# Loading W1 and W2 by 128-partition blocks from SyncE alone, and sharing the rounding of W1's first block with VectorE

## What is computed

```python
hidden = concat([cond, cond])                  # (4, 512)
x_mean = mean(x, axis=1, keepdims=True)        # over the 1024 rows of a batch
fused  = concat([x, x_mean, hidden])           # 1536 features for each row
out    = x + relu(fused @ W + b)               # W is (1536, 512)
```

## Time and profile before

| | us |
|---|---|
| median of the runs | 104.74 |
| the profiled execution | 105.25 |
| its span on the core | 103.1 |
| TensorE busy | 97.4 |
| VectorE busy | 81.7 |
| ScalarE busy | 47.3 |
| GpSimd busy | 41.0 |
| the first product that counts starts | 7.07 |
| `mean_bias(1)` starts | 40.57 |
| the last product starts | 99.50 |

### The profile page before, as it was taken

The page is one execution under the profiler, slowest core; times in us unless marked ns, Lnnn a source line. Parts: engine busy times, 40 slices in busy tenths (PEclk is TensorE's granted clock), DMA queues, the critical chain, the costliest instruction groups (busy, mean ns, idle before and its releaser), DMA issues.

```text
span 103.1 us, 1694 instructions
## 1 busy us (share of the span) xinstructions
PE 97.4 (95%) x523; PEld 78.3 (76%) x523; DVE 81.7 (79%) x146; ACT 47.3 (46%) x116; POOL 41.0 (40%) x37
## 2 busy tenths in 40 slices
PE   5989999999999898999999999999999999999970
PEld 2349999778888585888888886888888886888960
DVE  3173869979879999999999994999999994839660
ACT  3277426875606549777487100874744004610000
POOL 1029700000000000999857700468577059992000
PEclk9999999999999999999999999999999999999997
DMA  2999999999999999999999999300591690199995
GB/s 63 290 306 273 220 214 216 235 235 218 233 270 253 209 224 221 225 225 224 219 296 349 309 282 251 97 0 0 111 267 29 144 253 14 39 279 263 230 330 183
DMA packets 34990, 21.39 MB, mean 207 GB/s; under 512 B 1572, under 2 KB 32680, under 8 KB 34984
## 3 DMA queue, kind: packets, MB, share of 16 engines
q1 hardware_dynamic: 33400, 20.13, 85.4%
q10 hardware_dynamic: 1584, 1.18, 3.8%
HBM read 12.91 MB, written 8.39 MB: 207 GB/s over the span
## 4 chain that ended last, share of the span: by engine, by line
PE 57%; SPq 18%; DMA 10%; DVE 7%; issue 3%; ACT 1%; DVEq 0%
PE ps_y L457 46%; DMA xa<-in_x_dram 10%; SPq L162 9%; PE ps_y L558 4%; PE ps_y L560 4%; PE ps_y L559 4%; SPq L166 2%; SPq L170 2%; DVE w2x L361 2%; DVE ps_xt L331 2%; SPq L158 2%; SPq L195 2%; ACT xh L257 1%; DVE xl L337 1%; SPq L190 1%
## 5 line engine op out<-in xcount | busy, mean ns | idle before, releaser
L232 POOL TENSOR_TENSOR xa<-xa,back 128x512 f32 x28 | 35.6, 1295 | 45.8 <-DVE back L344 45.8
L457 PE MATMUL ps_y<-xh,w1h 128*128 (+2 forms) x128 | 43.7, 368 | 0.3 <-ACT w1h L250 0.3
L457 PE MATMUL ps_y<-xl,w1h 128*128 (+2 forms) x128 | 43.1, 363 | 0.0
L457 PE MATMUL ps_y<-xh,w1l 128*128 (+2 forms) x128 | 42.9, 363 | 0.0
L257 ACT ACTIVATE xh<-ps_xt 128x512 fp32r<-128x512 f32 (+1 forms) x36 | 19.7, 549 | 21.1 <-DVE ps_xt L331 21.1
L331 DVE STREAM_TRANSPOSE ps_xt<-xa 128x512 f32<-128x512 f32 (+1 forms) x36 | 22.3, 643 | 5.8 <-DMA xa<-in_x_dram 5.4
L457 PEld LDWEIGHTS ps_y<-xh,w1h 128*128 128x128 f32 x128 | 22.6, 188 | 5.6 <-issue 0.8
L457 PEld LDWEIGHTS ps_y<-xh,w1l 128*128 128x128 f32 x128 | 22.6, 189 | 3.9
L337 DVE TENSOR_TENSOR xl<-ps_xt,xh 128x512 fp32r<-128x512 f32 (+1 forms) x36 | 22.2, 618 | 4.1 <-ACT xh L257 4.1
L457 PEld LDWEIGHTS ps_y<-xl,w1h 128*128 128x128 f32 x128 | 22.7, 189 | 3.5
L275 ACT ACTIVATE relu_t<-ps_y,bias 128x512 f32<-128x512 f32 x20 | 13.5, 686 | 16.5 <-DVE bias L378 15.0
(11 more groups left out here) (34 smaller groups left out, 35.8 us busy)
## 6 DMA issues: line engine op xcount, KB each, us to landing
xa<-in_x_dram SPq DMA_DIRECT2D x28, 256.0 KB, 7.2
out_dram<-xa SPq DMA_DIRECT2D x28, 256.0 KB, 4.1
w<-in_L_cond_W_dram SPq DMA_DIRECT2D x4, 256.0 KB, 7.6
w<-in_L_cond_W_dram SPq DMA_DIRECT2D x2, 512.0 KB, 8.3
w<-in_x_dram SPq DMA_DIRECT2D x4, 256.0 KB, 6.2
out_dram<-w SPq DMA_DIRECT2D x3, 256.0 KB, 3.2
xa<-in_x_dram SPq DMA_DIRECT2D x4, 128.0 KB, 3.6
xa<-in_x_dram ACTq DMA_DIRECT2D x4, 128.0 KB, 4.0
```

What stands on the lines that cost most here:

```text
L232: nc.gpsimd.tensor_tensor(rows, rows, back[:, t], ALU.add).then_inc(added, 1)
L457: return nc.tensor.matmul(ps_y[:, t, ls], lhs, rhs, start=start, stop=stop, skip_group_check=True)
```

## The change

- `load_w1` and `load_w2` take a block k in place of a list of quadrants. One transfer of 256 KB fills all 128 partitions of block k, from `wv[0, :, :, k]`, an array of 4 by 32 rows of 512 numbers; the rows of one j follow each other, and those of the next j begin 128 rows further on. There are four transfers for W1 (12 before) and four for W2 (as before, but these had one j and all k each).
- SP alone issues W1 and the second part of x0. ACT issues only its half of x0's first part.
- x1 is issued ahead of the condition, and VectorE takes the transpose of the condition behind x1's pieces.
- Each block of W1 has a semaphore of its own, so block 2 no longer waits for block 3.
- ScalarE rounds only the first two of the four tiles of W1's block 0, and does so between x0's first two pieces; VectorE copies the other two (`tensor_copy`, 128x256). TensorE waits for these ahead of its tile 2, and GpSimd for both parts.
- `WARM` is 12 in place of 14.

```diff
-WARM = 14
+WARM = 12
...
+    DVE_T = NK // 2
...
-        def load_w1(eng, first, end, quadrants):
-            for j in quadrants:
-                eng.dma_start(w1[Q * j:Q * j + Q, first:end], wv[0, j, :, first:end]).then_inc(w1_landed[first], 16)
-
-        def load_w2(eng, quadrants):
-            for j in quadrants:
-                eng.dma_start(w2[Q * j:Q * j + Q], wv[1, j]).then_inc(w2_landed, 16)
+        def load_w1(eng, k):
+
+            eng.dma_start(w1[:, k], wv[0, :, :, k]).then_inc(w1_landed[k], 16)
+
+        def load_w2(eng, k):
+            eng.dma_start(w2[:, k], wv[1, :, :, k]).then_inc(w2_landed, 16)
...
             load_x0(sp, 0, LOW)
-            load_w1(sp, 0, 1, LOW)
-            load_w1(sp, 1, 2, LOW)
-            load_w1(sp, 2, NK, LOW)
-            load_x0(sp, 1, LOW)
+            for k in range(NK):
+                load_w1(sp, k)
+            load_x0(sp, 1, ORDER)
+            load_x(sp, 1, ORDER)
             sp.wait_ge(cond_zeroed, 1)
...
-            load_x(sp, 1, ORDER)
             load_x(sp, 2, ORDER)
-            load_w2(sp, ORDER)
+            for k in range(NK):
+                load_w2(sp, k)
...
             for k in range(NK):
-                pool.wait_ge(w1_landed[min(k, NK - 2)], 16 * NQ)
+                pool.wait_ge(w1_landed[k], 16)
                 pool.wait_ge(w1h_ready, k + 1)
+                if k == 0:
+                    pool.wait_ge(w1h_rest_ready, 1)
...
             nc.scalar.activation(act_warm[:], ones[:, 0:1], ACT.Relu)
-            load_w1(act, 0, 1, HIGH)
-            load_w1(act, 1, 2, HIGH)
-            load_w1(act, 2, NK, HIGH)
-            load_x0(act, 1, HIGH)
 
             def w1_high(k):
-                act.wait_ge(w1_landed[min(k, NK - 2)], 16 * NQ)
-                nc.scalar.activation(as_tiles(w1h[:, k]), by_tile(w1[:, k]), ACT.Copy).then_inc(w1h_ready, 1)
+                act.wait_ge(w1_landed[k], 16)
+                ts = slice(0, NK if k else DVE_T)
+                nc.scalar.activation(as_tiles(w1h[:, k])[:, ts], by_tile(w1[:, k])[:, ts], ACT.Copy).then_inc(w1h_ready, 1)
...
-            x_high(0)
-            x_high(1)
-            w1_high(0)
-            w1_high(1)
-            for k in range(2, NK):
+            for k in range(NK):
                 x_high(k)
                 w1_high(k)
...
             turn_x(0)
-            turn_and_split(0, pieces_to(1))
+            turn_x(1)
+            dve.wait_ge(w1_landed[0], 16)
+            nc.vector.tensor_copy(as_tiles(w1h[:, 0])[:, DVE_T:NK], by_tile(w1[:, 0])[:, DVE_T:NK]).then_inc(w1h_rest_ready, 1)
+            x_low(0)
+            turn_x(2)
+            turn_and_split(1, 2)
+            turn_and_split(2, pieces_to(1))
+            turn_x(pieces_to(1))
+            turn_and_split(pieces_to(1), pieces_to(H))
 
             dve.wait_ge(cond_landed, 16 * NQ)
             nc.vector.transpose(cond_t[:], cond_c[:].rearrange("p m k -> p k m")).then_inc(cond_spread, 1)
-            turn_x(pieces_to(1))
-            turn_and_split(pieces_to(1), pieces_to(H))
...
                     for t in range(NK):
+                        if half == 0 and k == 0 and t == DVE_T:
+                            pe.wait_ge(w1h_rest_ready, 1)
                         mm(t, ls, w1h[:, k, t], xh[:, 0, k, ls], start=(half == 0 and k == 0))
```

More of the change, by code:

```diff
@@ L135, in build @@
         x_landed = [sem(f"x_landed{g}") for g in range(G)]
-        w1_landed = [sem(f"w1_landed{k}") for k in range(NK - 1)]
+        w1_landed = [sem(f"w1_landed{k}") for k in range(NK)]
         w2_landed, w3_landed = sem("w2_landed"), sem("w3_landed")
@@ L140, in build @@
         warm_zeroed, cond_zeroed, ones_set = sem("warm_zeroed"), sem("cond_zeroed"), sem("ones_set")
-        w1h_ready, w1l_ready = sem("w1h_ready"), sem("w1l_ready")
+        w1h_ready, w1h_rest_ready, w1l_ready = sem("w1h_ready"), sem("w1h_rest_ready"), sem("w1l_ready")
         cond_spread, const_summed, const_ready = sem("cond_spread"), sem("const_summed"), sem("const_ready")
@@ L350, in mean_terms @@
                     nc.vector.tensor_tensor(xsum[:, 1], xsum[:, 0], xsum[:, 1], ALU.add).then_inc(halves_summed, 1)
-                    dve.wait_ge(w2_landed, 16 * NQ)
+                    dve.wait_ge(w2_landed, 16 * NK)
                     dve.wait_ge(halves_summed, 1)
```

## The result

Four runs of the changed kernel took 121.85 to 124.22 us, median 123.54; the kernel before, run beside it, 104.89. The ratio is 1.174, interval 1.168 to 1.179. Medians here are of all runs; ratios and their intervals leave out the runs over 1.5% above the fastest of their kernel. The profiled execution took 123.41 us (before 105.25), with a span of 121.6. The direction is the forecast one. The size is not: 18.65 us by the medians where 10 were forecast, outside the range.

A forecast was written before the change was run, and what follows sets the result against it. x3's landing, then fixed TensorE work, bounds the kernel. 4.2 + 22.4 + 13.3 + 0.5 lands x3 at 40.4, 9.5 later: 105.25 + 9.5 = 114.8, by the median 114.2, plus 0.5 for the clock: 114.7 (80% range 111.8 to 120.5).

The forecast's parts named there:

- Too few engines: Loads of W1 and W2: four runs in memory send each block through 4 engines, 64 KB each, not 16.
- 2.8 us a W block, 22.4 for eight: Loads ahead of x3: each W1 or W2 block takes 2.8 us on its four engines, eight 22.4 (21.5 to 28).
- twelve idle engines leave less crowding: Loads on the four engines: with the others idle or ahead, 2.8 us a W block and 3.8 a group of x.
- The group of x at 3.8 us: Loads up to x3: each group of x takes 3.8 us on one engine; 3.5 groups make 13.3 (12.2 to 16.8).
- The high end of my own working, 49.5: x3's landing: forecast at 40.4, range 38.4 to 49.5, against 30.9 before.
- the second rival: Loads: four engines, crowded as before, 3.5 us a block, 4.8 a group; up to 123.3, half way 119; 15 in 100.
- W3 lands near 43.5: W3's load behind x3, still on 16 engines: lands near 43.5 to 44, 43.5 taken; TensorE waits from 39.6.
- x3 decides: Mean product of batch 1: x3's landing plus 9.7 gives 50.1, TensorE's path through W3 49.1; x3 sets it by 1 us.
- The clock at 0.5 us on even chances: TensorE behind its wait for W3: a possible fall to 1.2 GHz, up to 2.6 us, was priced at 0.5.
- The third rival: TensorE behind the wait for W3: low clock adds 2.6 us, 116.8 in all, or 117.5; 13 in 100.
- The other edits at 0: Shared rounding, x1 ahead of the condition and issuing all from SP: all priced at 0 us.
- The 0.6 forecast for the start: TensorE's start: the small edits are worth 0.6 us there if the blocks spread over 16 engines after all.

The follow-up runs named there:

- The filled wait: The changed kernel with 31 products of zeroes on TensorE ahead of its wait for W3: 121.56 us.

## Why the forecast was right in kind and wrong in size

- **Too few engines: right, and shown.** 100 GB/s at a share of 0.26 for four runs, 50 for two, and no loss for one run of 128 rows; the landing notices count 2, 4, 8 and 16 engines for two, four and eight runs and one run of 128 rows. By the Trainium skill (DMA: Bandwidth & Descriptors, "Why a DMA increments its semaphore by 16 and not by 1") four engines carry such a block; the notices agree. The advice of the Trainium skill for one 128-partition transfer (same page, "Rules for kernel authors") holds here only where memory, too, has the rows in one run: 105.06 us against 123.54.
- **The step that failed first: 2.8 us a W block, 22.4 for eight.** It is right only where a block moves by itself (12.69 to 15.36: 2.7). The blocks landed at 9.2, 12.7, 15.4 and 19.2, forecast 7.4, 10.2, 13.0 and 15.8. 1.8 us of that come with the first block and its pause, 1.6 with the second and the fourth. I had written that twelve idle engines leave less crowding, and that put the slowing at next to nothing. The twelve are not idle while x0 and x1 pass on them, and W's packets take 0.12 to 0.17 us from 10.5 to 12 and 0.13 to 0.18 from 16 on, against 0.084. x does not queue on the four engines ahead of the blocks: its last 16 notices come behind them. What slows the four engines is not shown; it goes with traffic on the others, but not in every stretch (from 11.5 to 12 hardly a packet of x moves and W's are still slow, and from 9.0 to 9.75 x moves and W's keep their 0.084). W2 took 11.9 for 11.2, counted from x2's last notice at 29.87.
- **The group of x at 3.8 us.** x0's second half came 1.9 behind W1, as priced; x1 4.3 behind that, x2 4.5 behind x1, x3 5.55 behind W2 (b is between them). x3 is 6.95 late, 47.35 for 40.4: 3.4 from W1, 0.7 from W2, the rest from the groups. The high end of my own working, 49.5, held it. I took prices near the low end of each range; the second rival's half way was nearer.
- **"W3 lands near 43.5", and x3 decides: wrong.** Before, W3 came 3.6 behind x3; I took 3.1. It came 4.45 behind, at 51.8, and 2 us of this are x4's packets beside it. My sum let x3 decide by 1 us, and that order did not hold. From x3 the chain would have given 47.35 + 9.7 = 57.05; W3's gave 58.99. The two are not independent: VectorE makes the condition's row in its program order ahead of the mean's steps, and waits 0.74 us for TensorE there. The mean's steps end at 55.96 + 2.33 = 58.3, still 0.6 ahead of TensorE.
- **The clock at 0.5 us on even chances: undersized.** It was 0.50 from 48.4 to 55.2, and from W3 to the mean product 7.1 us passed, where the forecast had 5.6. The filled wait confirms 1.6. The third rival had 2.6 at the place, because I took 18 products at full 0.43; the clock was back before they ended. It was low at the start too: TensorE's first four products that count took 1.19 us where the earlier trace rows have 0.71.
- **The other edits at 0: right, and not for the stated reason in full.** With one-run blocks all of them stand, SP alone among them, and the time is 105.06. What SP alone can't do for nothing is 16 pieces of W1: those cost 3.2 us. No run takes the edits out beside the four-engine blocks. The 0.6 forecast for the start is seen in one profile and not in the times.
- **Slips in the working that change nothing.** From 35.75 to 40.57 there are 4.8 us, not 5.2; the 4.4 that is used is right. By its own terms x0's second half lands near 17.7, not 17.4. x3's last issue begins at 20.62 but ends at 23.8, so SP issues x3 from 18.14 to 23.8.

So the signs of the second rival (x3 later than 44) and of the third (a low clock behind W3) came on top of the forecast. I had priced crowding and the clock as alternatives to the main case, each from its own point; they were additions to it. By the dates at the mean product, 58.99 against 50.1 in my working without the clock's term, 6.95 us of the miss are x3's, and the other 1.9 are W3's lag and the clock.

## What to carry to other kernels

Before merging transfers into one over all partitions, look at the memory side: if the rows are not one run there, the count of runs decides how many engines carry it (here 2, 4 and 8), and a missing time to landing in the list of issues is its sign. A transfer that keeps a few engines busy also delays every later transfer that uses all of them, as x0's last 16 notices show. Behind the wait of 7.5 us TensorE worked at half clock on top, so price crowding and clock as parts of the sum. When a transfer becomes the bound, follow the last one in its queue, not the one that decided before.

## What the runs showed that I had not expected

- Four blocks of four runs, issued from 1.67 us on, move 23 GB/s from 4 to 6 us, and the first lands at 9.2; issued alike with one run each it lands at 6.6, and three engines of 16 are late there too.
- Two, four and eight runs for W2: landed at 51.2, 41.8 and 39.7 us. The number of engines doubles each time, the rate only from two to four.
- x4, issued behind W3 in the same queue, delays W3 by 2 us.
- SP's issues are held up when engines are late. SP's timeline in the changed kernel, the issues of W2, b and x3:

```profile
24.40 4.20 SPq L172 DMA_DIRECT2D w<-in_L_cond_W_dram  x4
28.65 4.12 SPq L197 DMA_DIRECT2D b_row<-in_L_cond_b_dram  x4
32.81 7.78 SPq L165 DMA_DIRECT2D xa<-in_x_dram  x4
```

And in the kernel before, the issues of x3:

```profile
18.14 5.68 SPq L162 DMA_DIRECT2D xa<-in_x_dram  x4
```

An issue that waits for nothing takes 0.42 us, four of them 1.7. Before, x3's took 5.68, so SP was held up there too; now they take 7.78, b's 4.12, and in the chain of waits SP's issues are 33% of the span. That a few late engines hold up the queue of all sixteen is how I read this; no run took it apart.
